# Two stacked attention layers over 32 images: other slots for the first layer's key-query projections, 64-row score products in the second

## The reference

```
h = group_norm(x, 32 groups, eps 1e-5) * gn_w + gn_b
q, k, v = split(qkv_w h + qkv_b)
x1 = x + proj_w (v softmax(q.T k / sqrt(128)).T) + proj_b
q1, k1, v1 = Wq x1 + bq, Wk x1 + bk, Wv x1 + bv      (q1, k1: 16 channels; v1: 128)
y  = x1 + gamma * (v1 softmax(q1.T k1).T)
```

## Time and profile before

| | |
|---|---|
| median of 3 runs | 1681.65 us (1681.08 to 1683.28) |
| profiled execution, its own time | 1683.15 us |
| its span in the profile | 1681.4 us |
| busy: TensorE, VectorE, ScalarE, GpSimd | 92%, 80%, 72%, 74% of the span |
| granted TensorE clock, mean | 0.985 of full speed |

### The profile page before, as it was taken

One profiled execution on the slowest core, in us unless ns is written; L12 is line 12 of the kernel. 1 busy time (PEld: TensorE's weight loads), 2 busy tenths in 40 slices (PEclk: granted clock), 3 DMA queues, 4 the chain that ended last, 5 costly groups with the idle time before them and its releaser, 6 DMA issues.

```text
span 1681.4 us, 43596 instructions
## 1 busy us (share of the span) xinstructions
PE 1539.8 (92%) x16777; PEld 1147.6 (68%) x16777; DVE 1344.3 (80%) x2547; ACT 1216.3 (72%) x1697; POOL 1249.7 (74%) x1039
## 2 busy tenths in 40 slices
PE   4889999999999999999999999999999999999865
PEld 2557777776777767777677777777767777677654
DVE  2578888888888888888888888888888888888853
ACT  2477777777777777777777777777777777777643
POOL 5997877877788777778777778778777887777500
PEclk9999999999999999999999999999999999999986
DMA  2699999999999999999999999999999999999954
GB/s 58 114 170 197 185 185 203 196 193 191 194 187 187 202 189 189 199 191 193 190 196 194 191 194 184 190 203 194 194 187 195 187 190 202 190 177 190 183 111 93
DMA packets 1081117, 305.20 MB, mean 182 GB/s; under 512 B 1067952, under 2 KB 1068624, under 8 KB 1080912
## 3 DMA queue, kind: packets, MB, share of 16 engines
q1 hardware_dynamic: 1079760, 302.41, 101.7%
q10 hardware_dynamic: 1152, 0.00, 0.0%
HBM read 17.13 MB, written 16.78 MB: 20 GB/s over the span
## 4 chain that ended last, share of the span: by engine, by line
PE 43%; ACT 26%; DVE 16%; issue 12%; POOL 2%; DMA 1%; ACTq 0%; POOLq 0%; DVEq 0%; SPq 0%
DVE nmax L493 9%; ACT scores L403 9%; ACT prob L398 8%; PE mixed L698 7%; PE mixed L700 7%; PE mixed L699 7%; PE scores L659 4%; PE scores L684 4%; PE bank_w L766 4%; ACT k_odd L432 3%; PE scores L661 3%; PE scores L660 3%; PE bank_t L719 3%; ACT v_head L450 2%; PE bank_w L756 2%
## 5 line engine op out<-in xcount | busy, mean ns | idle before, releaser
L698 PE MATMUL mixed<-v_head,pt 128*128 128x129 f16 x4096 | 724.8, 224 | 2.5 <-DMA pt<-rows 2.5
L700 PE MATMUL mixed<-v_head,pt 128*128 128x129 f16 x4096 | 724.5, 221 | 0.0
L699 PE MATMUL mixed<-v_tail,pt 128*128 128x128 f16 x4096 | 724.3, 220 | 0.0
L493 DVE TENSOR_REDUCE nmax<-scores 128x1 f32<-128x1024 f32 x512 | 602.9, 1217 | 64.7 <-PE scores L684 45.2
L306 POOL TENSOR_TENSOR rows<-prob,rows 128x1024 f16<-128x1024 f32 x256 | 545.0, 2129 | 21.4
L403 ACT ACTIVATE scores<-scores,nmax 128x1024 f32<-128x1024 f32 x256 | 278.6, 1088 | 343.1 <-DVE nmax L493 343.1
L301 POOL TENSOR_SCALAR rows<-prob 128x1024 f16<-128x1024 f32 x256 | 267.1, 1043 | 269.0 <-ACT prob L398 265.4
L507 DVE SCALAR_TENSOR_TENSOR rows<-scores,rows 128x1024 f16<-128x1024 f32 x256 | 313.5, 1225 | 153.0 <-ACT rows L410 153.0
L699 PEld LDWEIGHTS mixed<-v_tail,pt 128*128 128x128 f16 x4096 | 408.0, 100 | 2.9 <-issue 0.3
L698 PEld LDWEIGHTS mixed<-v_head,pt 128*128 128x128 f16 x4096 | 400.7, 98 | 5.0 <-DMA pt<-rows 3.9
L700 PEld LDWEIGHTS mixed<-v_head,pt 128*128 128x128 f16 x4096 | 398.8, 97 | 0.0
(11 more groups left out here) (93 smaller groups left out, 1922.8 us busy)
## 6 DMA issues: line engine op xcount, KB each, us to landing
x_raw<-in_x_dram SPq DMA_DIRECT2D x32, 512.0 KB, 4.7
out_dram<-y SPq DMA_DIRECT2D x64, 256.0 KB, 2.9
pt<-rows SPq DMA_TRANSPOSE x512, 4.7
w_qkv<-in_L_conv_qkv_w_dram SPq DMA_DIRECT2D x3, 64.0 KB, 3.9
w_proj<-in_L_conv_proj_w_dram SPq DMA_DIRECT2D x1, 64.0 KB, 3.8
w_v<-in_L_conv_Wv_dram SPq DMA_DIRECT2D x1, 64.0 KB, 3.6
b_qk<-in_L_conv_bk_dram SPq DMA_DIRECT2D x4, 0.1 KB, 2.2
b_qk<-in_L_conv_bq_dram SPq DMA_DIRECT2D x2, 0.1 KB, 3.0
```

The costliest lines, as they stand in the source:

```text
L493: nc.vector.reduce_max(nmax[layer][:, t:t + 1], scores[layer][:, :], AX.X, negate=True).then_inc(maxed[layer], 1)
L698: mm(mixed[l][:, 0:C + 1], head, vh[:, im.p, m, 0:C + 1], start=(m == 0), stop=False)
L699: mm(mixed[l][:, 0:C], head, vt[:, im.p, m, :], start=False, stop=False)
L700: done = mm(mixed[l][:, 0:C + 1], tail, vh[:, im.p, m, 0:C + 1], start=False, stop=(m == TILES - 1))
```

## The change

It does two things. The second layer's queries and keys get a new layout: all 128 rows of `bank_w` hold keys in one half and queries in the other, the halves exchanged between the first and the second half of the image; ScalarE writes one masked copy of 128 rows, VectorE one difference of 128 rows, and ScalarE copies 64 rows of queries over to the other half (`qk1_copy`, one slot later, ahead of the second layer's exponential). The score of a tile is then one product of rows 0 to 63 for the first 512 columns and one of rows 64 to 127 for the last. And offsets change: the first layer's two key projections from slots 3 and 4 to 1 and 2, their split with them, the group statistics from 4 and 5 to 1 and 2, their small steps from 6 and 7 to 3 and 4, their root on GpSimd from 0 to 5, the normalised image from 1 and 2 to 6 and 7, `x_bias` from 3 to 4, `x1_bias` from 7 to 5. The setup has 29 loads in place of 19, and more small copies.

```diff
@@ -35,8 +35,9 @@
 SWING = (1, 13)
 ATTEND = (3, 16)
 ADD = (4, 17)
-QK_AT = (-5, -4, -3, 0)
-GN_AT = (-10, -9)
+QK_AT = (-7, -6, -3, 0)
+SPLIT_AT = (-6, -5, -2, 1)
+GN_AT = (-13, -12)
 V_AT = (1, 2)
 QK1_AT = (7, 11)
 V1_AT = (12, 14)
@@ -138,8 +140,8 @@
         v_tail = sb("v_tail", [C, 2, TILES, C], F16)
         x1 = sb("x1", [C, 2, N])
         x1b = sb("x1b", [C, 2, N])
-        qk1 = sb("qk1", [C, 2, 2, N], F16)
-        k_odd = sb("k_odd", [C, HALF], F16)
+        qk1 = sb("qk1", [C, 2, 3, HALF], F16)
+        qk1_masked = sb("qk1_masked", [C, HALF], F16)
         v1_head = sb("v1_head", [C, 2, TILES, VW], F16)
...
@@ -260,20 +262,19 @@
                       (w1_qk[CQK:2 * CQK, :], Wk)]
             for dst, src in loads:
                 sp.dma_start(dst, src).then_inc(setup_loaded, 16)
-            sp.wait_ge(zeroed, 1)
-            for r, src in ((0, bq), (16, bq), (64, bk), (80, bk), (96, bk), (112, bk)):
-                sp.dma_start(b1_qk[r:r + CQK, :], col(src)).then_inc(setup_loaded, 16)
+            for h in range(2):
+                for r in range(8):
+                    src = bk if (r < 4) == (h == 0) else bq
+                    sp.dma_start(b1_qk[r * CQK:(r + 1) * CQK, h:h + 1], col(src)).then_inc(setup_loaded, 16)
             every_iteration(body)
             for h in range(2):
...
@@ -367,17 +367,17 @@
 
             def body(it):
                 for k in range(8):
-                    if im := at(it, k, -8):
+                    if im := at(it, k, -11):
                         gn_root_out(im)
-                    if im := at(it, k, -7):
+                    if im := at(it, k, -10):
                         h_full(im)
-                    if im := at(it, k, -6):
+                    if im := at(it, k, -9):
                         h_tail_out(im)
-                    if im := at(it, k, 15):
+                    if im := at(it, k, 13):
                         x1_bias(im)
-                    if im := at(it, k, -5):
+                    if im := at(it, k, -4):
                         x_bias(im)
-                    for j, offset in enumerate((-4, -3, -2, 1)):
+                    for j, offset in enumerate(SPLIT_AT):
                         if im := at(it, k, offset):
                             qk_split(im, j)
                     if tile := tile_at(it, k, EXP[0]):
@@ -424,13 +424,16 @@
                 nc.scalar.activation(qk32[:, s, h, :], bank_t[:, :], ACT.Identity, bias=bias[:, 0:1],
                                      scale=scale).then_inc(qk_out, 1)
 
-            def qk1_head_out(im, h):
-                cols = slice(h * HALF, (h + 1) * HALF)
+            def qk1_mask_out(im, h):
                 act.wait_ge(qk1_made, im.n * 2 + h + 1)
-                nc.scalar.activation(qk1[0:32, im.p, Q_SIDE, cols], bank_w[0:32, :], ACT.Identity,
-                                     bias=b1_qk[0:32, 0:1], scale=1.0).then_inc(qk1_headed, 1)
-                nc.scalar.activation(k_odd[64:128, :], bank_w[64:128, :], ACT.Identity,
-                                     bias=b1_odd[64:128, 0:1], scale=odd[64:128, 0:1]).then_inc(qk1_headed, 1)
+                nc.scalar.activation(qk1_masked[:, :], bank_w[:, :], ACT.Identity, bias=b1_masked[:, h:h + 1],
+                                     scale=masks[:, h:h + 1]).then_inc(qk1_headed, 1)
+
+            def qk1_copy(im, h):
+                act.wait_ge(qk1_tailed, im.n * 2 + h + 1)
+                queries, copy = ((slice(64, 128), slice(0, 64)), (slice(0, 64), slice(64, 128)))[h]
+                nc.scalar.activation(qk1[copy, im.p, 2, :], qk1[queries, im.p, h, :],
+                                     ACT.Copy).then_inc(qk1_copied, 1)
 
             def h_head_out(im):
                 act.wait_ge(gn_root, im.n * ROOT_STEPS + ROOT_STEPS)
@@ -453,6 +456,9 @@
 
             def body(it):
                 for k in range(8):
+                    for h in range(2):
+                        if im := at(it, k, QK1_AT[h] + 1):
+                            qk1_copy(im, h)
                     if tile := tile_at(it, k, EXP[1]):
                         exponent1(*tile)
                         head_row1(*tile)
@@ -462,13 +468,13 @@
                         if im := at(it, k, V_AT[h]):
                             v_head_out(im, h)
                         if im := at(it, k, QK1_AT[h]):
-                            qk1_head_out(im, h)
+                            qk1_mask_out(im, h)
                         if im := at(it, k, V1_AT[h]):
                             v1_head_out(im, h)
                     for j in range(4):
                         if im := at(it, k, QK_AT[j]):
                             qk_copy_out(im, j)
-                    if im := at(it, k, -7):
+                    if im := at(it, k, -10):
                         h_head_out(im)
                     for l in range(2):
                         if tile := tile_at(it, k, ATTEND[l]):
...
@@ -554,14 +560,9 @@
                                         ALU.mult).then_inc(gn_dve, 1)
 
             def qk1_tail_out(im, h):
-                cols = slice(h * HALF, (h + 1) * HALF)
-                dve.wait_ge(qk1_headed, im.n * 4 + h * 2 + 1)
-                nc.vector.scalar_tensor_tensor(out=qk1[32:64, im.p, Q_SIDE, cols], in0=bank_w[0:32, :],
-                                               scalar=b1_qk[0:32, 0:1], in1=qk1[0:32, im.p, Q_SIDE, cols],
-                                               op0=ALU.add, op1=ALU.subtract)
-                dve.wait_ge(qk1_headed, im.n * 4 + h * 2 + 2)
-                nc.vector.scalar_tensor_tensor(out=qk1[0:64, im.p, K_SIDE, cols], in0=bank_w[64:128, :],
-                                               scalar=b1_qk[64:128, 0:1], in1=k_odd[64:128, :], op0=ALU.add,
+                dve.wait_ge(qk1_headed, im.n * 2 + h + 1)
+                nc.vector.scalar_tensor_tensor(out=qk1[:, im.p, h, :], in0=bank_w[:, :], scalar=b1_qk[:, h:h + 1],
+                                               in1=qk1_masked[:, :], op0=ALU.add,
                                                op1=ALU.subtract).then_inc(qk1_tailed, 1)
 
             def v_tail_out(im, h):
@@ -594,18 +595,30 @@
                 nc.vector.tensor_scalar(w1_v_t[:, :], scores[0][:, 3 * C:4 * C], gam[:, 0:1], 1.0, ALU.mult,
                                         ALU.mult).then_inc(setup_dve, 1)
                 dve.wait_ge(setup_pe, 5)
-                dve.wait_ge(consts_made, 10)
-                for r, s in ((0, 0), (16, 0), (64, 1), (80, 1), (96, 1), (112, 1)):
-                    done = nc.vector.tensor_copy(w1_qk_t[:, r:r + CQK], scores[1][:, s * CQK:(s + 1) * CQK])
+                dve.wait_ge(consts_made, 8)
+                for h in range(2):
+                    for r in range(8):
+                        src = CQK if (r < 4) == (h == 0) else 0
+                        done = nc.vector.tensor_copy(w1_qk_t[:, h, r * CQK:(r + 1) * CQK],
+                                                     scores[1][:, src:src + CQK])
                 done.then_inc(setup_dve, 1)
...
@@ -640,7 +653,7 @@
                             qk1_tail_out(im, h)
                         if im := at(it, k, V1_AT[h]):
                             v1_tail_out(im, h)
-                        if im := at(it, k, -12 + h):
+                        if im := at(it, k, -15 + h):
                             gn_first(im, h)
                     if im := at(it, k, GN_AT[0]):
                         gn_second(im)
@@ -677,12 +690,12 @@
                 if t or im.at_least(1):
                     pe.wait_ge(row_tailed[1], im.n * TILES + t)
                 if t == 0:
-                    pe.wait_ge(qk1_tailed, im.n * 2 + 2)
-                ns = slice(t * C, (t + 1) * C)
-                for h in range(2):
-                    cols = slice(h * HALF, (h + 1) * HALF)
-                    done = mm(scores[1][:, cols], qk1[:, im.p, Q_SIDE, ns], qk1[:, im.p, K_SIDE, cols],
-                              start=True, stop=True)
+                    pe.wait_ge(qk1_copied, im.n * 2 + 2)
+                half, ns = t // PER_HALF, slice((t % PER_HALF) * C, (t % PER_HALF + 1) * C)
+                for h, low in enumerate((slice(0, 64), slice(64, 128))):
+                    queries = half if h != half else 2
+                    done = mm(scores[1][:, h * HALF:(h + 1) * HALF], qk1[low, im.p, queries, ns],
+                              qk1[low, im.p, h, :], start=True, stop=True)
                 done.then_inc(scored[1], 1)
 
             def attend(l, im, t):
@@ -723,11 +736,10 @@
                 if j == 0:
                     pe.wait_ge(h_tail_done, im.n + 1)
                     pe.wait_ge(h_head_done, im.n + 1)
-                if j == 3:
-                    if im.before(-1).exists():
-                        pe.wait_ge(gn_dve, im.n * GN_STEPS + 2 * GN_STEPS)
-                elif j or im.at_least(1):
+                if j or im.at_least(1):
                     pe.wait_ge(qk_out, im.n * 4 + j)
+                if j == 2 and im.before(-1).exists():
```

(34 more changed lines are left out.)

29 lines of the change are left out of this document (13 added, 16 removed).

## The result

| | before | after |
|---|---|---|
| median | 1681.37 us (1680.17 to 1683.28, 4 runs) | 1654.85 us (1652.01 to 1655.33, 4 runs) |
| ratio | | 0.9838, 95% interval 0.9821 to 0.9855 |
| profiled execution, span | 1683.15, 1681.4 us | 1652.01, 1649.9 us |
| granted TensorE clock | 0.985 | 0.987 |

The account below looks back on a forecast made before the run. A loop over engines, not one engine, was taken to set the pace. Slots summed to 49.14 against 49.43 a round, -8.5 us, and the ends -1.5: 1673.1 profiled, 1671.6 us forecast, range 1664 to 1679.

Parts of the forecast that it names:

- X, S and M: Starts of first-layer exponential, next first-layer score product, second-layer row maximum; shortest slot 1.16 + 1.29 + 3.36 = 5.81 us.
- the copy of queries at nothing: ScalarE's added copy before the exponential of slots 0 and 4 costs nothing; uncovered, 0.77 twice a round.
- the start: Ten more small loads before the setup and ten more copies: between 0 and +7 us, taken as +3.5.
- the ends: Start of the run, +3.5 us, and its last rounds, -5 us: together -1.5.
- a: What the pair of 64-row products adds to S + 1.29, the second-layer maximum's earliest start: -0.05 us.
- b: What the pair of 64-row products adds to S + 1.96, the start of TensorE's attention: +0.10 us.
- X + 1.00 + 0.77 + 0.04 + 0.77 = X + 2.58: Slots 3 and 7, merged evictions: M can be at X + 2.58 instead of X + 3.44 and about 3.35.
- the second half with the aggregate 1.04: VectorE's second half-image of statistics with the aggregate takes 1.04 us; in slot 2 it gives M = X + 3.27.
- 1 (complete overlap at no price, 1653.6): Pair of 64-row products overlaps completely, no switch price: -0.91 a round, 1653.6 us; chance 0.22.
- 2 (serial): The pair runs one after the other, two switches a slot: 1691 us at 0.14 each, 1740 at 0.33; chance 0.18.
- 3 (a wait in slots 1 or 2): Moves cost more than they give through an unseen wait, 0.3 a round: 1681 us, no change; chance 0.14.
- 4 (the pair does nothing to TensorE): The pair changes nothing, a = b = 0: 49.1 a round, the forecast's time; chance 0.46 together with the forecast.

Follow-up runs that it names:

- e11: The new layout with the old offsets, with the added copy of queries made twice: 1640.33 us, ratio 0.9743 to the kernel before.
- e4: The changed kernel with both 64-row score products on rows 0 to 63: 1675.34 us, ratio 0.9952 to the kernel before.
- e8: The changed kernel with the head behind the norms on ScalarE, three image buffers and statistics in slots 5 and 0: 1631.11 us, ratio 0.9695 to the kernel before.

## Why the prediction was right and wrong

**Right:** the direction; the loop through X, S and M; that slot 2 becomes the dearest of the moved ones with statistics and aggregate ahead of its maximum, and slot 7 the longest; that slots 0, 4 and 5 end alike; the copy of queries at nothing (e11); the start, +3.0 where +3.5 was taken. The two products of the pair start together, and the weight loads have gaps before and after them, as was said. At the start the added small loads take 0.46 each, and TensorE waits for the last of them:

```profile
6.39 3.66 SPq L268 DMA_DIRECT2D b_qk<-in_L_conv_bq_dram  x8
...
13.11 0.66 PE L799 MATMUL scores<-ident,w_qkv 128*128 128x128 f32 x2 [4.49 <-DMA b_qk<-in_L_conv_bk_dram]
```

**Wrong:** the size, so the predicted sum. Against the profiled execution 1673.1 was forecast and 1652.0 came. The steady state makes 0.65 a round of it, 18.9 us over 29.1 rounds, and the ends, -1.5 forecast, about -4. The terms:

1. "I take 0.14 for each switch, the nearest row, and the second product 0.03 behind the first: a = -0.05, b = +0.10." Measured a = -0.10, b = -0.01. The 0.14 was read at the slow clock (in the kernel before, products of 512 columns stand 0.43 apart until 37 us, and 0.22 in the steady state, where the granted clock is 0.985; the profile's windows read 1.00 for that early stretch too), for 32 rows of float32; at the fast clock a switch to 64 rows of float16 and back costs 0.10 each way. Slots 0, 4 and 5: 0.05 each, 0.15. The cost b wasn't there either, so TensorE ends the value projections earlier: ScalarE copies them at X + 1.00 in slot 1 and X + 1.28 in slot 6, where 1.07 and 1.34 were taken. Slot 1: M at X + 2.84, not X + 2.91, 6.19 for 6.27. Slot 6: 5.87 for 5.93. 0.29 together.
2. "X + 1.00 + 0.77 + 0.04 + 0.77 = X + 2.58." The last 0.77 was the pitch of a 64-row difference (the time from its start to the next step's). Of 128 rows it is 0.67: slot 3 6.27 for 6.38, slot 7 6.54 for 6.65. "Width in rows costs nothing" was right in sign, but the wider one is the quicker to hand over. 0.22 together.
3. "the second half with the aggregate 1.04": 0.95 here (761.28 to 762.23). The earlier trace rows was misread: its maximum at 789.73 did not wait for the aggregate but for the scores, since S of that slot plus 1.29 is 789.73.

```profile
788.44 0.39 PE L659 MATMUL scores<-qk_head 128*128 128x512 f16 x1 [0.41 <-ACT prob L398]
```

From this M to the next X it is 3.31, not 3.36; why is not known. Slot 2: 6.50 for 6.63, 0.13.

0.29 + 0.22 + 0.13 = 0.64. Each is a tenth of a microsecond, all point one way, and a forecast of -0.29 a round, as a small difference of large terms (+1.12 in slots 1 and 2, -1.41 in the others), could not bear them. So the mechanism held, and what failed is the size of these three terms: the price of the switches, the hand-over of the 128-row difference, and the statistics with their aggregate.

**The rivals.** 1 (complete overlap at no price, 1653.6) hit the time for the wrong reason: slots 0, 4 and 5 are 5.71, not 5.60 to 5.67. 2 (serial) is what e4 is: slots 0, 4 and 5 are 5.92 where 5.95 was worked out, and the time is 1675, not 1691, mostly by terms 2 and 3 above and the cheaper switch. 3 (a wait in slots 1 or 2) did not come. 4 (the pair does nothing to TensorE) is true of b, not of a. The rule weighed in the prediction, the Trainium skill, TensorEngine Tiling (Array Packing), Key Properties, that changing the tiling mode drains the engine: the traces agree, 0.10 at each change, and in e4 the weight loader is idle for 0.42 before the two 64-row products and for 0.42 behind them. The Trainium skill, TensorE: Matmul & The Clock Gate, Part 3, says that products of different row groups run together: the traces agree here too, 0.39 for both against 0.60 in e4.

A step that was missing: I costed the change only as a whole. By the same rows the moves alone would probably have shown as a loss (the forecast itself had +1.12 in slots 1 and 2), and the question which edit carries the gain would have led to the merged evictions and to their pitch.

## What to carry to other kernels

Where an engine's evictions stand ahead of the instruction that sets the pace, count instructions, not rows: cutting one copy and one difference of 128 rows into two of 64 each cost 0.91 of a slot of 6. Two 64-row products in a stream of 128-row ones just broke even here on TensorE (0.21 saved by running together, 0.20 for the two switches), and the gain was in when the result was ready. A step moved off a long slot lands in another: look at the order on the engine there (a copy for a later image ahead of the norms cost 16 to 19 us in slot 6, and nothing in slot 1), and undo each part alone before keeping it. The best kernel here, e8, keeps the layout and the other moves, has the head behind the norms, and the statistics in slots 5 and 0, which are short.
